# Expert up products from rounded parts and rests, with a re-ordered drain and routing chain

## The chip, the cores and the metric

One core of a Trainium2 chip. The metric is the device time of one execution in microseconds (us). An execution's time is its span, from the first to the last instruction, and a little around it.

## What is computed

A decoder layer in float32 for x of 16 batches x 256 tokens x 256 features:

1. Stage A: causal self-attention (16 heads, relative position bias, RMS norms) with a ReLU network 256-1024-256.
2. Stages B and D: attention to a context (8 heads, layer norms), then a second ReLU network, 256-1024-256, in stage D.
3. Stage C: each of the 4096 tokens takes the nearest of 8 centroids, and goes through that expert alone:

```python
xn = rms_norm(x)
ids = argmin(dist2(xn, centroids))
h = xn @ up_w[e]                   # 256 -> 1024, e the token's expert
a, g = split(h, 2)                 # 512 each
y = (a * silu(g)) @ down_w[e]      # 512 -> 256
out = y + x
```

## The kernel before

The kernel is written per engine: each engine has its own queue, run in order, and semaphores order them against each other. Phase 1 is a software pipeline over the batches: `PHASES` (line 131) lists turns, and in one turn stage A works on one batch, B on the one before, D on the one before that, C on the one before that. Within a turn the order of the attention pieces is the list `PLAN` (lines 77 to 81), which every engine walks, skipping the stages that its turn hasn't got. The last turns have fewer stages: B + 1 has B, D, C; B + 2 has D and C (D of batch 15, C of batch 14); B + 3 has C alone. These three are the drain.

What matters of the drain, by engine. VectorE: `rest` (L1122) makes the second part of a value, the difference between it and its rounded copy; D.out is taken at L1335 and goes through statistics (L1134, L1137), scaling (L1344, L1350), statistics again; the scaled rows begin at L1269; `nearest` (from L1181 to L1194) picks the expert. ScalarE: L737 rounds D's input (`d_qT_hi`), `hidden` (L754, L755) takes the hidden halves of D's network from PSUM, `scaled_rows` (L729) stands between its second and third call. GpSimd: `layer_then_rms` (L933 to L955) computes two norms from the statistics in ten operations of 2 elements. TensorE: D's hidden products are made from rounded parts and rests already (`split_cols_out`): with w = w_hi + w_low and x = x_hi + x_low, three single-pass products x_hi w_hi, x_hi w_low, x_low w_hi stand for one product in float32, which takes two passes. Eight eighths of D.out ("out", and two after the plan) share PSUM bank 5 with D.h2, so the first waits for the third `hidden`.

The experts' weights (8 x 1 MB up, 8 x 0.5 MB down) are loaded in turn B + 1, into the room of stage A.

Routing follows the drain: GpSimd makes counters (L1020 to L1024), VectorE runs a chain of small operations on the experts of all 4096 tokens (L1429 to L1473), in which every step waits for the one before, and TensorE sorts the tokens by expert with one-hot products: `in_row` (L1459) says which row in a tile a token takes, `in_tile` (L1455) which tile, and `number` (GpSimd L1030, ScalarE L867) is what is sorted. All three engines first wait for `phase1_over`: the last expert chosen and the last rows stored.

The expert stage has 39 tiles of 128 tokens, two a step, in 19 steps and one lone tile. For a tile GpSimd gathers the rows (L1035), TensorE transposes them (L1844), ScalarE copies them from PSUM (L871), TensorE makes the up products in two halves of 512 columns (`up_half`, in float32), ScalarE takes Silu of one half (L876), VectorE multiplies by the other (L1482), TensorE transposes the hidden values (L1869), ScalarE copies them (L878), TensorE makes the down products, VectorE adds the token's own row (L1493), and GpSimd scatters the result (L1056). `product` (L1505) records nearly all matrix products, so tiles and not lines tell them apart.

Of the kernel before, what the change touches and what calls it, by code (L numbers as in the profile page):

```python
# [31 lines left out]
P = 128  # L32
# [7 lines left out]
E = 8  # L40
# [40 lines left out]
PLAN += [("out", "D", 5), ("weigh", "B", 1), ("norm", "A", 0), ("norm", "A", 1), ("norm", "B", 0), ("norm", "B", 1)]  # L81

# [84 lines left out]
def _build(nc, d, ctx):  # L167
# [77 lines left out]

    b_kh, b_kl, b_qh, b_ql = (sbuf(ctx, name, [P, C, S], F32R) for name in ("b_kh", "b_kl", "b_qh", "b_ql"))
# [6 lines left out]
    def carver():  # L253

        at = [0]
# [21 lines left out]
    w1o = p1("w1o", [P, C, D])  # L277
    w11 = p1("w11", [P, C, HID])
    w12 = p1("w12", [P, J, D])
# [8 lines left out]

    rec = p1("rec", [P, 3, S])
    rec_few = p1("rec_few", [P, 16])  # L290
    x1 = p1("x1", [P, T, D])

    c_in = p1("c_in", [P, T, D])
    b_ctxT = p1("b_ctxT", [P, C, S])
    b_xl = p1("b_xl", [P, T, D])
    b_xT = p1("b_xT", [P, C, S])


    b_v = p1("b_v", [P, T, D])
    b_nm = p1("b_nm", [P, T, C, 4, 32])  # L300
    b_p = p1("b_p", [P, NPB, T, S])
    b_zT = p1("b_zT", [P, C, S])
    b_yT = p1("b_yT", [P, C, S])
    b_q = p1("b_q", [P, T, D])
    b_hT = p1("b_hT", [P, J, S])
# [211 lines left out]
    s_route, s_pp, s_wmoe = map(sem, ("routing_chain", "prefixes_made", "experts_loaded"))  # L517
# [13 lines left out]
    pr.close()  # L531
    up = sbuf(ctx, "up", [P, E, C, 2 * EH])
    down = sbuf(ctx, "down", [P, E, EJ, D])
    p3 = carver()
    m_row = p3("m_row", [P, 2, 2, 1], U32)
    m_token = p3("m_token", [P, 2, 1], U32)
    m_in = p3("m_in", [P, 2, D])
    m_skip = p3("m_skip", [P, 2, D])
    m_xT = p3("m_xT", [P, 2, C, P])
    m_sg = p3("m_sg", [P, 2, EH])  # L540
    m_h = p3("m_h", [P, 2, EH])
    m_hT = p3("m_hT", [P, 2, EJ, P])
    m_out = p3("m_out", [P, 2, D])
    oh = p3("oh", [P, NT, E])
    r_pp = p3("r_pp", [P, NT, E])
# [17 lines left out]
    r_id = p3("r_id", [P, 4, TILES_MAX])  # L563
    io_p = p3("io_p", [P, 1])
    io_r = p3("io_r", [P, P])
    io_n = p3("io_n", [P, NT])
    io_e = p3("io_e", [P, E])
    io_t = p3("io_t", [P, NT])
    io_i = p3("io_i", [P, TILES_MAX])
    tri = p3("tri", [P, P])  # L570
    ones_nt = p3("ones_nt", [P, NT])
    s_iota, s_numbered = sem("iotas_made"), sem("one_hot_numbered")
    BY_TILE = {"m_loaded": 16, "m_skip": 16, "m_row": 1, "m_x": 1, "m_xT": 1, "m_up": 1, "m_silu": 1,
# [33 lines left out]
    def _(sp):  # L607
# [23 lines left out]
        def load_experts():  # L631

            after(sp, "b_xl", B - 1)
            for e in range(E):
                sp.dma_start(up[:, e], w_view(d["L0_ffn_up_w"][e])).then_inc(s_wmoe, 16)
                sp.dma_start(down[:, e], w_view(d["L0_ffn_down_w"][e])).then_inc(s_wmoe, 16)
# [47 lines left out]
    def _(act):  # L684
# [29 lines left out]

        def evacuate(it, job, dst, view=None):

            src = full(act, it, job)[:]
            copy(dst, src if view is None else view(src)).then_inc(e_sem(job), 1)  # L718

        def turn(it):  # L720
# [83 lines left out]
            for what, st, n in PLAN:  # L804
                if st not in it.stages:
                    continue
                if what == "lengths":
                    after(act, "c_rows", c, T)
                    for t in range(T):
                        nc.scalar.activation(b_zT[:, t], c_rows[:, t, 0:D], ACT.Square,  # L810
# [56 lines left out]
        nc.scalar.activation(number[:, :, 1], in_tile[:], ACT.Copy, scale=io_p[:, 0:1]).then_inc(s_numbered, 1)  # L867
# [22 lines left out]
    def _(pool):  # L890
# [125 lines left out]
        phase1_over(pool)  # L1016
        for io, pattern, base, by_partition in (
# [12 lines left out]
        pool.tensor_tensor(number[:, :, 0], in_tile[:], io_n[:].unsqueeze(2).to_broadcast([P, NT, TILES_MAX]),  # L1030
                           ALU.mult).then_inc(s_numbered, 1)
# [7 lines left out]
        pool.wait_ge(s_route, ROUTE_ALL)  # L1039
        for u in range(2):  # L1040
# [30 lines left out]
    def _(dve):  # L1071
# [101 lines left out]
        def turn(it):  # L1173
# [57 lines left out]
            if Dd:  # L1231
# [56 lines left out]
            for what, st, n in PLAN:  # L1288
# [127 lines left out]
        phase1_over(dve)  # L1416
        dve.wait_ge(s_iota, 8)
# [56 lines left out]
        assert link[0] == ROUTE_ALL  # L1474

# [469 lines left out]
```

## Time and profile before

| | us |
|---|---|
| runs (3) | 1348.08, 1350.71, 1352.39; median 1350.71 |
| profiled execution, its own time | 1350.49 |
| span of the profiled execution | 1348.80 |
| TensorE busy in the span | 1223.9 (91%) |
| VectorE, ScalarE, GpSimd busy | 811.2, 611.4, 413.7 |
| mean granted clock of TensorE, share of full | 0.959 |

PE is TensorE, PEld its weight loads, DVE VectorE, ACT ScalarE, POOL GpSimd. In a row, "128x512 f32<-128x512 f32" is output and input shape, "x4" how many instructions a row merges, and the bracket says how long the engine had been idle and who released it. Times are from the start of the span.

### The profile page before, as it was taken

What the parts mean: (1) busy time and instruction counts of PE and PEld (TensorE: products, weight loads), DVE (VectorE), ACT (ScalarE), POOL (GpSimd) and SP (SyncE); (2) the same over time, 40 slices, a digit from 0 to 9 for tenths busy, and PEclk for the clock granted to TensorE, in tenths of its full rate; (3) what the DMA queues carried; (4) which work ended last, traced back from release to release, by engine and by line L of the source; (5) the groups of instructions that cost most, each with busy time, mean ns of one, the idle gap of its engine ahead of it and who ended that gap; (6) DMA issues with size and microseconds to landing.
All of it is one profiled execution on the core that took longest, in us unless ns stands there. A gap on an engine that the chain in (4) does not pass through costs nothing.

```text
span 1348.8 us, 29314 instructions
## 1 busy us (share of the span) xinstructions
PE 1223.9 (91%) x9542; PEld 915.5 (68%) x9543; DVE 811.2 (60%) x2110; ACT 611.4 (45%) x1288; POOL 413.7 (31%) x712
## 2 busy tenths in 40 slices
PE   6497999999999999999999999999985289999997
PEld 4274778778787877878787787878765145555554
DVE  3737667777786877778687777877644611211211
ACT  3426456464746646474654647465442122222211
POOL 1310324233142423314142331414122234444352
PEclk9598999999999999999999999999998589999998
DMA  8402520303213030321303032130383012121121
GB/s 265 126 1 110 222 107 17 111 16 109 80 52 117 16 109 16 109 80 48 121 16 109 16 109 77 48 124 9 111 324 113 16 49 64 51 62 53 55 66 28
DMA packets 51768, 112.29 MB, mean 83 GB/s; under 512 B 7333, under 2 KB 38863, under 8 KB 44944
## 3 DMA queue, kind: packets, MB, share of 16 engines
q1 hardware_dynamic: 45456, 96.81, 21.3%
q0 software_dynamic: 5616, 14.43, 3.6%
q10 hardware_dynamic: 656, 0.52, 0.1%
q8 instruction: 24, 0.39, 0.1%
q14 instruction: 16, 0.13, 0.0%
HBM read 89.72 MB, written 22.94 MB: 84 GB/s over the span
## 4 chain that ended last, share of the span: by engine, by line
PE 76%; DVE 10%; ACT 6%; issue 5%; DMA 2%; POOL 1%; SPq 0%; DVEq 0%; ACTq 0%; POOLq 0%
PE bank L1505 69%; PE bank L1540 3%; DVE a_p L1295 2%; PE bank L1706 2%; ACT shared L823 2%; PE bank L1869 1%; DMA rows_skip<-shared 1%; ACT shared L878 1%; ACT a_p L818 1%; DVE b_ql L1199 1%; DVE a_split L1227 1%; DVE a_split L1226 1%; DVE a_split L1225 1%; DVE a_ss L1236 1%; ACT a_sq L741 1%
## 5 line engine op out<-in xcount | busy, mean ns | idle before, releaser
L1505 PE MATMUL bank<-shared 128*128 128x256 f32 (+4 forms) x1730 | 320.3, 376 | 27.6 <-POOL shared L1030 11.3
L1505 PEld LDWEIGHTS bank<-shared 128*128 128x128 f32 (+2 forms) x1730 | 219.8, 166 | 88.7 <-issue 31.7
L1295 DVE TENSOR_TENSOR a_p<-a_p,eb 128x385 f32<-128x385 f32 x256 | 125.9, 555 | 75.6 <-ACT a_p L818 75.6
L1505 PE MATMUL bank<-up,shared 128*128 x312 | 143.8, 604 | 11.1 <-issue 11.1
L991 POOL TENSOR_SCALAR a_rz<-a_ms 128x2 f32<-128x2 f32 x16 | 3.1, 191 | 407.5 <-ACT a_sq L842 407.5
L818 ACT ACTIVATE a_p<-bank 128x385 f32<-128x385 f32 x256 | 105.1, 504 | 44.3 <-PE bank L1505 44.2
L1482 DVE TENSOR_TENSOR shared<-bank,shared 128x512 f32<-128x512 f32 x39 | 27.0, 692 | 153.7 <-ACT shared L876 153.7
L1505 PEld LDWEIGHTS bank<-up,shared 128*128 128x128 f32 x312 | 56.9, 192 | 75.6 <-issue 75.6
L876 ACT ACTIVATE shared<-bank 128x512 f32<-128x512 f32 x39 | 23.3, 597 | 137.2 <-PE bank L1505 137.2
L1505 PE MATMUL bank<-down,shared 128*128 x312 | 76.8, 390 | 7.2 <-ACT shared L878 7.2
L823 ACT ACTIVATE shared<-bank 128x512 f32<-128x512 f32 x128 | 66.1, 603 | 35.3 <-PE bank L1505 35.3
L1262 DVE TENSOR_REDUCE shared<-bank 128x2 f32<-128x512 f32 x128 | 79.4, 684 | 1.3 <-PE bank L1505 1.3
L1505 PEld LDWEIGHTS bank<-down,shared 128*128 128x128 f32 x312 | 58.2, 192 | 27.2 <-issue 20.9
L971 POOL TENSOR_TENSOR a_split<-a_sq,a_split 128x256 f16<-128x256 f32 x64 | 42.8, 699 | 104.6 <-ACT a_split L772 104.6
L1035 POOL DMA_INDIRECT shared<-rows_x,shared x35 | 33.1, 945 | 112.1 <-PE bank L1844 107.0
L1505 PE MATMUL bank<-a_p,a_v 128*32 128x256 f32 (+1 forms) x1024 | 58.5, 347 | 8.0 <-DVE a_p L1295 6.2
L1505 PE MATMUL bank<-w_low,a_hT_hi 128*128 128x256 f32 x224 | 63.4, 283 | 0.0
L1505 PE MATMUL bank<-w_hi,a_hT_hi 128*128 128x256 f32 x224 | 62.9, 281 | 0.0
L1505 PE MATMUL bank<-d_qT_hi,w_hi 128*128 128x256 f32 x256 | 57.4, 306 | 5.8 <-DVE d_qT_low L1122 5.8
L1505 PE MATMUL bank<-w_hi,a_hT_low 128*128 128x256 f32 x224 | 62.4, 279 | 0.0
L1505 PE MATMUL bank<-w0qk,a_xnT 128*128 128x512 f32 x128 | 61.1, 621 | 0.7 <-ACT a_xnT L718 0.7
L927 POOL TENSOR_TENSOR shared<-shared,mhalf 128x2 f32<-128x2 f32 x80 | 56.3, 704 | 12.7 <-POOL shared L959 6.6
(237 smaller groups left out, 2724.8 us busy)
## 6 DMA issues: line engine op xcount, KB each, us to landing
w_low<-low_w SPq DMA_DIRECT2D x44, 1024.0 KB, 4.8
up<-in_L_ffn_up_w SPq DMA_DIRECT2D x8, 1024.0 KB, 13.9
x_in<-in_x SPq DMA_DIRECT2D x16, 256.0 KB, 2.7
shared<-in_ctx SPq DMA_DIRECT2D x16, 256.0 KB, 3.1
rows_x<-shared SPq DMA_DIRECT2D x16, 256.0 KB, 5.8
rows_skip<-shared SPq DMA_DIRECT2D x16, 256.0 KB, 6.2
down<-in_L_ffn_down_w SPq DMA_DIRECT2D x8, 512.0 KB, 12.3
toep<-a_hT SPq DMA_DIRECT2D x1, 3072.0 KB, 10.2
```

The costliest lines, as they stand in the source:

```text
L818: nc.scalar.activation(a_p[:, head % NPA], ps[:, 0:SCOLS], ACT.Exp).then_inc(e_sem(f"A.s{head}"), 1)
L823: nc.scalar.activation(b_p[:, head % NPB].rearrange("p t s -> p (t s)"), ps[:], ACT.Exp).then_inc(e_sem(f"B.s{head}"), 1)
L876: nc.scalar.activation(m_sg[:, u], bank[3 + 2 * u][:], ACT.Silu).then_inc(mig[u]["m_silu"], 1)
L927: pool.tensor_tensor(out, in_, mhalf[:, 0:out.shape[-1]], ALU.pow).then_inc(sig[name], 1)
L971: ins = pool.tensor_tensor(a_split[:, t, H0:, slot, :], hat[:, H0:], a_split[:, t, H0:, 0, :], ALU.subtract)
L1035: pool.indirect_dma_start(out=dst[:, u], out_offset=None, in_=src.ap(), in_offset=bass.IndirectOffsetOnAxis(ap=rows, axis=0)).then_inc(mig ...
L1262: dve.tensor_reduce(b_nm[:, n // 4, :, n % 4, 0:1], ps[:].rearrange("p (m s) -> p m s", s=S), AX_X, ALU.max, negate=True).then_inc(e_sem(f ...
L1295: tt(a_p[:, n_ % NPA], a_p[:, n_ % NPA], eb[:, n_], ALU.mult).then_inc(sig["a_p"], 1)
L1482: tt(m_h[:, u], bank[2 + 2 * u][:], m_sg[:, u], ALU.mult).then_inc(mig[u]["m_h"], 1)
L1505: return mm(out, lhsT=lhsT, rhs=rhs, start=first, stop=last, **kw)
L1540: ins = nc.tensor.transpose(ps[:, c * S + t * P:c * S + (t + 1) * P], x[:, t, c * P:(c + 1) * P], ident[:])
L1706: ins = nc.tensor.transpose(ps[:, g * P:(g + 1) * P], a_split[:, t, h:h + 2].rearrange("p h s d -> p (h s d)"), ident16[:])
```

## The change

- Every up weight is kept as a rounded part `up_hi` and a rest `up_low`, the latter in the place of the weights. ScalarE rounds (`round_up_weights`), VectorE subtracts (`rest_of_up`, in halves of 128 x 1024). The parts for experts 0 to 2 are rounded at the start of turn B + 2, 3 to 6 at its end, 7 after D.out; the rests of experts 0 to 3 stand in VectorE's turn B + 2 between `nearest` and D.out, 4 and 5 after the last statistics of that turn, 6 and 7 after the routing chain.
- Each tile's transposed rows become `m_xhi` (ScalarE) and `m_xlow` (VectorE), and an up half is six products of rounded operands in place of two in float32.
- The rest of D's input for batch 15 moves from the start of turn B + 2 to turn B + 1, ahead of D.out of batch 14.
- Turn B + 2 walks `DRAIN_PLAN`, with the distances behind the third and fourth eighth of D.out.
- The counters have memory of their own and no longer wait for the end of phase 1; VectorE's routing waits for the last expert only, GpSimd's gathers for the stores.
- One-hot rows are made token column by token column (32 operations, 128 x 128 float16) rather than in four; `number` comes in two halves.
- Memory of phase 1 is laid out in another order, so that `up_hi` finds room.

```diff
+DRAIN_PLAN = [("lengths", "C", 0), ("out", "D", 0), ("out", "D", 1), ("rows", "C", 0), ("out", "D", 2), ("out", "D", 3)]
+DRAIN_PLAN += [("distances", "C", 0), ("expert", "C", 0), ("out", "D", 4), ("out", "D", 5)]
+def plan_of(turn):
+    return DRAIN_PLAN if turn.first == B + 2 else PLAN
...
+        def round_up_weights(which):
+            for e in which:
+                act.wait_ge(s_up[e], 16)
+                copy(flat(up_hi[:, e]), flat(up[:, e])).then_inc(s_up_hi, 1)
...
             if Dd:
                 copy(flat(d_qT_hi[:]), full(act, it, "D.q")[:]).then_inc(sig["d_qhi"], 1)
+            if it.first == B + 2:
+                after(act, "x1_kept", B - 1)
+                round_up_weights(range(3))
...
+            if it.first == B + 2:
+                after(act, "c_nx", c)
+                round_up_weights(range(3, E - 1))
+                taken(act, it, "D.out")
+                round_up_weights(range(E - 1, E))
...
-            copy(m_xT[:, u].rearrange("p c s -> p (c s)"), bank[u][:, 0:C * P]).then_inc(mig[u]["m_xT"], 1)
+            copy(flat(m_xhi[:, u]), bank[u][:, 0:C * P]).then_inc(mig[u]["m_xT"], 1)
...
-        phase1_over(pool)
...
+        pool.tensor_copy(io_r16[:], io_r[:]).then_inc(s_iota, 1)
...
+        for half in range(2):
+            part = slice(half * NT // 2, (half + 1) * NT // 2)
+            pool.tensor_tensor(number[:, part, 0], in_tile[:, part],
+                               io_n[:, part].unsqueeze(2).to_broadcast([P, NT // 2, TILES_MAX]),
+                               ALU.mult).then_inc(s_numbered[half], 1)
...
         pool.wait_ge(s_route, ROUTE_ALL)
+        phase1_over(pool)
...
+        def rest_of_up(halves):
+            for n in halves:
+                e, c_ = n // C, n % C
+                if c_ == 0:
+                    dve.wait_ge(s_up_hi, e + 1)
+                ins = tt(up_low[:, e, c_], up[:, e, c_], up_hi[:, e, c_].bitcast(F32), ALU.subtract)
+            ins.then_inc(s_up_low, len(halves) // C)
...
-            if Dd:
+            if Dd and it.first != B + 2:
                 rest(it, "D.q", d_qT_low[:], d_qT_hi[:], "d_qhi")
...
+            if it.first == B + 1:
+                rest(Turn(it.phase + 1, 0), "D.q", d_qT_low[:], d_qT_hi[:], "d_qhi")
...
+            if it.first == B + 2:
+                rest_of_up(range(0, 8))
             if Dd:
                 ps = full(dve, it, "D.out")
...
+            if it.first == B + 2:
+                rest_of_up(range(8, 12))
...
-        phase1_over(dve)
-        dve.wait_ge(s_iota, 8)
+        after(dve, "c_expert", B - 1)
+        dve.wait_ge(s_iota, 9)
...
-            chain(tt(in_row[:, part], bc(r_place[:, 1, part], P), over(io_r[:], NT // QUARTERS, P), ALU.is_equal))
+            for n in range(part.start, part.stop):
+                ins = ts(in_row[:, n], io_r16[:], r_place[:, 1, n:n + 1], None, ALU.is_equal)
+            chain(ins)
...
+        rest_of_up(range(12, 16))
+        def rest_of_rows(k, u):
+            after_tile(dve, "m_xT", k, u)
+            tt(flat(m_xlow[:, u]), bank[u][:, 0:C * P], flat(m_xhi[:, u]).bitcast(F32), ALU.subtract
+               ).then_inc(mig[u]["m_xl"], 1)
+        for u in range(2):
+            rest_of_rows(0, u)
...
                 tt(m_out[:, u], bank[DOWN_BANK[u]][:, 0:D], m_skip[:, u], ALU.add).then_inc(mig[u]["m_out"], 1)
+                if u == 0:
+                    for v in range(nxt):
+                        rest_of_rows(k + 1, v)
...
-        pe.wait_ge(s_wmoe, 16 * 2 * E)
+        pe.wait_ge(s_wmoe, 16 * E)
+        pe.wait_ge(s_up_low, E)
...
-            def up_half(u, half):
-                for c in range(C):
-                    w = up[:, bass.ds(expert[u], 1), c, half * EH:(half + 1) * EH]
-                    ins = product(bank[2 + 2 * u + half][:], m_xT[:, u, c], w.rearrange("p o n -> p (o n)"),
-                                  c == 0, c == C - 1)
+            def up_half(u, half, x_low_new):
+                for x, w_part in ((m_xhi, up_hi), (m_xhi, up_low), (m_xlow, up_hi)):
+                    if x is m_xlow and x_low_new:
+                        after_tile(pe, "m_xl", k, u)
+                    for c in range(C):
+                        w = w_part[:, bass.ds(expert[u], 1), c, half * EH:(half + 1) * EH]
+                        ins = product(bank[2 + 2 * u + half][:], x[:, u, c], w.rearrange("p o n -> p (o n)"),
+                                      c == 0 and x is m_xhi and w_part is up_hi, c == C - 1 and x is m_xlow)
```

## Rows read from the trace of the kernel before

**Rows 1.** The page, section 4: shares of the chain that ended last, by engine.

```profile
PE 76%; DVE 10%; ACT 6%; issue 5%; DMA 2%; POOL 1%; SPq 0%; DVEq 0%; ACTq 0%; POOLq 0%
```

**Rows 2.** Stretches: start:end, us, then busy us (instructions) per engine, clock, DMA, GB/s.

```profile
1022.00:1026.00 4.00, 1.60 (x7) 1.60 (x8) 2.31 (x7) 0.00 (x0) 1.75 (x6) 0.50 0.00 0
...
1257.40:1270.50 13.10, 12.16 (x44) 7.24 (x44) 2.62 (x11) 2.92 (x6) 5.89 (x7) 1.00 0.17 51
```

**Rows 3.** Timeline, one pair: start us, us, engine, line, op, out<-in, xcount [idle before].

```profile
1257.42 5.41 PE L1505 MATMUL bank<-up,shared 128*128 x12 [0.60 <-issue]
...
1262.67 0.60 PE L1869 MATMUL bank<-ident,shared 128*128 128x128 f32 x4
...
1264.83 1.89 PE L1505 MATMUL bank<-down,shared 128*128 x8
...
1266.56 0.60 PE L1869 MATMUL bank<-ident,shared 128*128 128x128 f32 x4
...
1267.03 0.42 DVE L1493 TENSOR_TENSOR shared<-bank,shared 128x256 f32<-128x256 f32 x1
...
1267.92 1.99 PE L1505 MATMUL bank<-down,shared 128*128 x8 [0.33 <-ACT shared L878]
...
1270.56 0.69 PE L1505 MATMUL bank<-up,shared 128*128 x1 [0.65 <-issue]
```

**Rows 4.** Timeline of TensorE, D.h of batch 15, three of its rows of two.

```profile
1026.70 0.63 PE L1505 MATMUL bank<-d_qT_low,w_hi 128*128 128x256 f32 x2
...
1027.92 0.40 PE L1505 MATMUL bank<-d_qT_hi,w_hi 128*128 128x256 f32 x2
...
1031.22 0.40 PE L1505 MATMUL bank<-d_qT_low,w_hi 128*128 128x256 f32 x2
```

**Rows 5.** Timeline of ScalarE and of VectorE, weights rounded and parted at the start.

```profile
130.00 1.93 ACT L713 CAST made<-w 128x2048 fp32r<-128x2048 f32 x1
...
134.49 2.28 DVE L1111 TENSOR_TENSOR a_hT_low<-w,a_hT_low 128x2048 fp32r<-128x2048 f32 x1
```

**Rows 6.** Timeline of the drain, batches 14 and 15, all engines.

```profile
1017.82 0.68 DVE L1335 TENSOR_TENSOR shared<-bank,shared 128x512 f32<-128x512 f32 x1
...
1018.66 0.58 ACT L737 CAST d_qT_hi<-bank 128x512 fp32r<-128x512 f32 x1 [8.70 <-PE bank L1540]
...
1023.67 0.67 DVE L1122 TENSOR_TENSOR d_qT_low<-bank,d_qT_hi 128x512 fp32r<-128x512 f32 x1
...
1027.55 2.96 DVE L1269 SCALAR_TENSOR_TENSOR shared<-shared 128x256 f32<-128x256 f32 x2 [3.20 <-POOL shared L955]
...
1031.83 1.99 PE L1505 MATMUL bank<-shared 128*128 128x256 f32 x8 [0.22 <-ACT shared L755]
...
1036.99 0.17 DVE L1194 CAST expert_of<-shared 128x2 f32<-128x2 uint32 x1
...
1041.38 0.69 DVE L1335 TENSOR_TENSOR shared<-bank,shared 128x512 f32<-128x512 f32 x1 [4.22 <-PE bank L1505]
...
1046.58 0.30 DVE L1137 BATCH_NORM_AGGREGATE shared<-shared 128x2 f32<-128x6 f32 x2
...
1050.68 0.88 DVE L1269 SCALAR_TENSOR_TENSOR shared<-shared 128x256 f32<-128x256 f32 x2 [3.80 <-POOL shared L955]
```

**Rows 7.** Timeline of the routing, all engines.

```profile
1056.88 0.17 DVE L1194 CAST expert_of<-shared 128x2 f32<-128x2 uint32 x1
...
1059.27 0.43 DVE L1429 TENSOR_TENSOR shared<-expert_of,shared 128x256 f32<-128x256 f32 x1 [2.21 <-POOL shared L1024]
...
1069.70 6.97 DVE L1459 TENSOR_TENSOR shared<-shared 128x1024 f16<-128x1024 f32 x4
...
1069.82 3.25 POOL L1030 TENSOR_TENSOR shared<-shared 128x1248 f16<-128x1248 f32 x1 [10.68 <-DVE shared L1455]
...
1079.10 0.18 DVE L1473 CAST sorted_row<-shared 128x39 uint32<-128x39 f32 x1
...
1082.78 0.66 PE L1844 MATMUL bank<-ident,shared 128*128 128x128 f32 x2 [5.36 <-DMA shared<-rows_x,sorted_row]
```

More of the change, by code:

```diff
@@ L251, in _build, with carver @@
     place = {}
-    def carver():
-        at = [0]
+    def carver(first=0):
+        at = [first]
         def carve(name, shape, dt=F32):
@@ L277, in _build @@
     w1o = p1("w1o", [P, C, D])
+    rec = p1("rec", [P, 3, S])
+    rec_few = p1("rec_few", [P, 16])
+    x1 = p1("x1", [P, T, D])
+    c_in = p1("c_in", [P, T, D])
+    b_ctxT = p1("b_ctxT", [P, C, S])
+    b_xl = p1("b_xl", [P, T, D])
+    b_xT = p1("b_xT", [P, C, S])
+    b_v = p1("b_v", [P, T, D])
+    b_nm = p1("b_nm", [P, T, C, 4, 32])
     w11 = p1("w11", [P, C, HID])
+    b_p = p1("b_p", [P, NPB, T, S])
+    b_zT = p1("b_zT", [P, C, S])
+    b_yT = p1("b_yT", [P, C, S])
+    b_hT = p1("b_hT", [P, J, S])
     w12 = p1("w12", [P, J, D])
@@ L514, in each @@
                     body(Turn(phase, k))
-    s_route, s_pp, s_wmoe = map(sem, ("routing_chain", "prefixes_made", "experts_loaded"))
+    s_route, s_pp, s_wmoe = map(sem, ("routing_chain", "prefixes_made", "down_weights_loaded"))
+    s_up = [sem(f"up_weights_loaded{e}") for e in range(E)]
+    s_up_hi, s_up_low = sem("up_weights_rounded"), sem("up_weights_rest_made")
     pa.close()
@@ L531, in _build @@
     pr.close()
+    under_up = ExitStack()
+    up_low = sbuf(under_up, "up_low", [P, E, C, 2 * EH], F32R)
+    under_up.close()
     up = sbuf(ctx, "up", [P, E, C, 2 * EH])
     down = sbuf(ctx, "down", [P, E, EJ, D])
[L534 to L543, printed above, removed]
+    m_xhi = sbuf(ctx, "m_xhi", [P, 2, C, P], F32R)
+    m_xlow = sbuf(ctx, "m_xlow", [P, 2, C, P], F32R)
+    UP_HI_END = E * C * 2 * EH - 5 * C * S
+    p3 = carver(UP_HI_END)
+    r_id = p3("r_id", [P, 4, TILES_MAX])
+    moe = carver(UP_HI_END + 160)
+    m_row = moe("m_row", [P, 2, 2, 1], U32)
+    m_token = moe("m_token", [P, 2, 1], U32)
+    m_in = moe("m_in", [P, 2, D])
+    m_skip = moe("m_skip", [P, 2, D])
+    m_sg = moe("m_sg", [P, 2, EH])
+    m_h = moe("m_h", [P, 2, EH])
+    m_hT = moe("m_hT", [P, 2, EJ, P])
+    m_out = moe("m_out", [P, 2, D])
     oh = p3("oh", [P, NT, E])
-    r_pp = p3("r_pp", [P, NT, E])
     r_tot = p3("r_tot", [P, NT, E])
@@ L560, in _build @@
     number = p3("number", [P, NT, 2, TILES_MAX], F16)
[L563 to L573, printed above, removed]
+    io_p = sbuf(ctx, "io_p", [P, 1])
+    io_r = sbuf(ctx, "io_r", [P, P])
+    io_n = sbuf(ctx, "io_n", [P, NT])
+    io_e = sbuf(ctx, "io_e", [P, E])
+    io_t = sbuf(ctx, "io_t", [P, NT])
+    io_i = sbuf(ctx, "io_i", [P, TILES_MAX])
+    io_r16 = sbuf(ctx, "io_r16", [P, P], F16)
+    tri = sbuf(ctx, "tri", [P, P])
+    ones_nt = sbuf(ctx, "ones_nt", [P, NT])
+    s_iota, s_numbered = sem("iotas_made"), [sem(f"one_hot_numbered{half}") for half in range(2)]
+    BY_TILE = {"m_loaded": 16, "m_skip": 16, "m_row": 1, "m_x": 1, "m_xT": 1, "m_xl": 1, "m_up": 1, "m_silu": 1,
                "m_h": 1, "m_ht": 1, "m_hT": 1, "m_down": 1, "m_out": 1, "m_stored": 16}
@@ L803, in turn @@
                 evacuate(it, "B.max", b_nmT[:].rearrange("p c s -> p (c s)"))
-            for what, st, n in PLAN:
+            for what, st, n in plan_of(it):
                 if st not in it.stages:
@@ L809, in turn @@
                     for t in range(T):
-                        nc.scalar.activation(b_zT[:, t], c_rows[:, t, 0:D], ACT.Square,
+                        junk = b_f if it.first == B + 3 else b_zT
+                        nc.scalar.activation(junk[:, t], c_rows[:, t, 0:D], ACT.Square,
                                              accum_out=c_nx[:, t:t + 1]).then_inc(sig["c_nx"], 1)
@@ L866, in _ @@
         act.wait_ge(s_route, ROUTE_IN_TILE)
-        nc.scalar.activation(number[:, :, 1], in_tile[:], ACT.Copy, scale=io_p[:, 0:1]).then_inc(s_numbered, 1)
+        for half in range(2):
+            part = slice(half * NT // 2, (half + 1) * NT // 2)
+            nc.scalar.activation(number[:, part, 1], in_tile[:, part], ACT.Copy, scale=io_p[:, 0:1]
+                                 ).then_inc(s_numbered[half], 1)
         def transposed(k, u):
             after_tile(act, "m_x", k, u)
-            copy(m_xT[:, u].rearrange("p c s -> p (c s)"), bank[u][:, 0:C * P]).then_inc(mig[u]["m_xT"], 1)
+            copy(flat(m_xhi[:, u]), bank[u][:, 0:C * P]).then_inc(mig[u]["m_xT"], 1)
         def step(k, n, nxt, nxt2):
@@ L1028, in _ @@
         pool.wait_ge(s_iota, 8)
+        pool.tensor_copy(io_r16[:], io_r[:]).then_inc(s_iota, 1)
         pool.wait_ge(s_route, ROUTE_IN_TILE)
-        pool.tensor_tensor(number[:, :, 0], in_tile[:], io_n[:].unsqueeze(2).to_broadcast([P, NT, TILES_MAX]),
-                           ALU.mult).then_inc(s_numbered, 1)
+        for half in range(2):
+            part = slice(half * NT // 2, (half + 1) * NT // 2)
+            pool.tensor_tensor(number[:, part, 0], in_tile[:, part],
+                               io_n[:, part].unsqueeze(2).to_broadcast([P, NT // 2, TILES_MAX]),
+                               ALU.mult).then_inc(s_numbered[half], 1)
         def gather(dst, src, rows, name, u):
@@ L1287, in turn @@
                 low_parts((0,))
-            for what, st, n in PLAN:
+            for what, st, n in plan_of(it):
                 if st not in it.stages:
@@ L1735, in out_eighth @@
                     ins.then_inc(f_sem("D.out"), 1)
-            for what, st, n in PLAN:
+            for what, st, n in plan_of(it):
                 if st not in it.stages:
```

31 lines of the change are left out of this document (11 added, 20 removed).

## The prediction

> **What bounds the kernel now.** I read the page's chain first: TensorE holds 76% of it [rows 1]. I then cut the span by stage, since the change touches only two: the expert stage (from 1085 us to the end) and the drain ahead of it (1017 to 1085 us), and read both as timelines.
>
> In the expert stage a pair of tiles takes 1270.56 - 1257.42 = 13.14 us, of which TensorE is busy 12.16 at full granted clock [rows 2, 3]. Up products are 16 of the 44 records: an fp32 product leaves two records, one per pass, and in the run of 12 they start every (5.41 - 0.69) / 11 = 0.43 us. So a 512-column up product costs 0.86 us, and a pair has 8 of them: 6.9 of 13.1 us.
>
> In the drain TensorE mostly waits. The chain goes from engine to engine: D.out, two norms on VectorE and GpSimd, the scaled rows on ScalarE, the transposes, the distances, the expert's choice, then the routing chain on VectorE [rows 6, 7]. There an instruction added to VectorE costs time wherever the chain isn't elsewhere.
>
> **The expert stage.** Each fp32 up product becomes three rounded ones: 24 instead of 16 records a pair. Their price isn't in the trace at 512 columns. Two rows bound it. A rounded 256-column product starts every (1031.22 - 1027.92) / 28 = 0.118 us, 14 rows of two in that stretch [rows 4]; two of them would be 0.236. An fp32 pass over 256 columns takes (1266.56 - 1264.83) / 8 = 0.216 us [rows 3]; since the rounded product is about twice as quick per column, 512 rounded columns occupy the array as long as one such pass. I take 0.216 (the nearer row: same array time per instruction), with 0.236 as the far end and 0.213 as the near one (512 columns at the upper clock level of 2.4 GHz).
>
> Not all of the saving lands. The order is up of tile 0 (12 products now), up of half of tile 1 (6), transposes of tile 0's hidden, the other half of tile 1 (6), down of tile 0. From the end of tile 0's up (1257.42 + 8 x 0.43 = 1260.86) through Silu, the gating multiply and the weight load to those transposes at 1262.67 there are 1.81 us; the half of tile 1 filled 1.72 of it. It shrinks to 6 x 0.216 = 1.30, but the hand-off stays 1.81, so TensorE waits about 0.5 us, and that half saves nothing. On the path: 12 x 0.43 = 5.16 becomes 18 x 0.216 = 3.89, a saving of 1.27 a pair. The second hand-off, tile 1's Silu and multiply, is still covered by the 1.73 us of tile 0's down. The rest of the period (1.36 from the second transposes to down of tile 1, then 2.64 to the next pair) is unchanged. 19 pairs x 1.27 = 24.1, plus the lone last tile's 8 x 0.43 - 12 x 0.216 = 0.85: **25.0 us less**. At 0.236: 19 x 0.91 + 0.6 = 17.9; at 0.213: 26.
>
> The rows' rests are new on VectorE: two operations of 256 elements from PSUM a pair, 0.42 us each like the output's [rows 3], put right after tile 0's output. VectorE is busy 2.62 of 13.1 us [rows 2], it waits there for down of tile 1, and the rests are wanted only at the fifth product of the next pair. I cost them at nothing; uncovered they would be 0.84 us a pair. The slack of GpSimd's six transfers a pair shrinks by 1.3 us, but GpSimd is busy only 5.9 of 13.1 [rows 2].
>
> **The drain, step by step.**
> 1. The rest of D.q (batch 15) goes ahead of D.out of batch 14 on VectorE. It waits for ScalarE's copy, which ends at 1018.66 + 0.58 = 1019.24, and takes 0.67 [rows 6]; D.out of 14 starts near 1019.9 instead of 1017.82. A store wait of 0.4 further down is absorbed, so its norm chain is **1.6 us** later. TensorE's D.h start 4 us earlier, and gain nothing: the last of the hidden halves stand behind the scaled rows of batch 14 on ScalarE, and D.out needs the bank that they free. D.out starts at 1031.83 + 1.6.
> 2. ScalarE rounds three experts ahead of the hidden halves: 3 x 1.93 = 5.8 us from 1019.24 [rows 5], done by 1025.1; scaled rows come after 1029. Hidden; with no cover, up to 5.8.
> 3. TensorE then stands idle some 5 us before D.out. In 1022 to 1026, where it had been idle too (busy 1.60 of 4.00), the granted clock was 0.50, the lower level of 1.2 GHz [rows 2], and two rounded products still took 0.63 instead of 0.40 at 1026.70 [rows 4]. I charge **1.3** (0 to 1.5). The distances now stand behind two more eighths of D.out: **0.6**. The choice of expert for batch 14 ends at 1036.99 + 0.17 + 1.6 + 1.3 + 0.6 = 1040.7.
> 4. Only then VectorE parts four experts: eight halves of 2.28 / 2 = 1.14 us each [rows 5], 9.1 us, up to 1049.8. These stand ahead of D.out of batch 15, whose products are done near 1043. It began at 1041.38, after 4.22 us of idleness [rows 6]. So **+8.4**: the 9.1 us are hidden only in part.
> 5. Two more experts are parted (4.6 us) between the last statistics (1046.58 + 0.30) and the next VectorE step at 1050.68, where GpSimd's ten small operations run, 3.8 us [rows 6]. Alone that costs 0.7. But a VectorE operation with two SBUF operands and a GpSimd one block each other here: the pair of L1269 that took 0.88 us at 1050.68 took 2.96 beside GpSimd's multiplications at 1027.55, and four one-hot quarters took 6.97 beside GpSimd's 3.25 us [rows 6, 7]. If each half lets one small operation through, the first four of the ten are pushed out to 5.9 us and the other 2.1 follow: 8.0 instead of 3.8, **+4.2**.
>
> The Trainium skill ("SBUF — State Buffer", Who interferes with whom) says the same as those rows: the pair of ports that VectorE and GpSimd share is locked for a whole instruction. It adds that a tensor_scalar may enter a mode that takes both ports, while writing DMA descriptors isn't held up by tensor_tensor. The first speaks against the one-hot rows of step 7, the second for the rests of step 8; no row here shows either. With both taken at the page's word the sum of the drain would be 11.9.
>
> 6. The iotas and the wait for batch 15's stores leave the path: 1059.27 - 1057.05 = **2.2 less** [rows 7].
> 7. One-hot rows: four operations (6.97 us, 2.0 of it blocked) become 32 short ones. Their price is unseen: between 0.1 and 0.25 us each, or 3.5 to 8, and GpSimd's numbering (now two halves) may block them twice. What follows is the same, so -3.5 to +1.1; I take **-0.5**, the blocked case being the nearer row.
> 8. The last two experts (4.6 us) stand between the last routing step (1079.28) and the first transposes, 3.5 us later [rows 7]; the rests of the first rows follow. 0.4 to 2.5, I take **+1**.
>
> Sum of the drain: 8.4 + 4.2 - 2.2 - 0.5 + 1 = **10.9 us more**; bounds 2.5 (no lower clock, no blocking, cheap rows) and 14.
>
> The profiled execution took 1350.49 (span 1348.80 and 1.69 around it), 0.2 under the median of 1350.71. 1350.5 - 25.0 + 10.9 = **1336 us**.
>
> **Rivals.**
> - No blocking on the shared port. Step 5 costs 0.7, step 7 gives 2.1, step 8 costs 0.4: drain +5.2, 1331 us. For: the ten GpSimd operations have two elements each, and none of them is seen beside such a long VectorE operation. Against: the two blocked rows.
> - A rounded 512-column product costs 0.236: 1350.5 - 17.9 + 10.9 = 1344. For: the 256-column ones are 0.01 above half of the fp32 pass, whatever that is; against: a cost per instruction wouldn't double with the columns.
> - Slower: the products become bound by their addresses. Each up product takes its weights at the expert's register, so the queue of TensorE computes an address for each, three times as many as now. With t per product, 19 x 18 + 12 = 354 on the path give 354 x (0.287 - t); the gain is eaten by the drain at t = 0.256. At 0.30 the time would be 1350.5 + 4.7 + 10.9 = 1366. For: nothing now runs at under 0.43 per address. Against: between 1267.92 and 1270.56 the queue computed three such addresses, read two expert numbers and took the loop's branch, with only 0.65 idle [rows 3].
> - The rests are covered on both sides but the drain takes all (no change): step 4 would have to cost 22 us, for which VectorE's rows leave no room.
>
> **How the numbers follow.** Forecast 0.55, no blocking 0.22, 0.236 a product 0.10, address-bound 0.08, the rest between. The range runs from 1324 (26 saved, drain near its lower bound) to 1347 (17.9 saved, drain at 14). A difference of 0.3%, 4 us, is what this measurement can tell from no change; the first three cases are all faster: 0.87 faster, 0.06 the same, 0.07 slower.
>
> **What would show it.** Up products of 0.216 apart in threes and a pair of 11.9 us with 0.5 us of TensorE waiting for VectorE ahead of the hidden transposes; D.out of batch 15 on VectorE near 1050, right behind the eight halves; GpSimd's small operations after it stretched by about 4 us; the routing's first step at once after the choice; first up products near 1096. A pair of 13 us or more would overturn the forecast, and so would halves that run before the distances are in.

## The result, and the profile after

The changed kernel takes **1356.49 us** (median of 6 runs, 1356.03 to 1358.61); the kernel before, beside it, 1349.53 (1347.57 to 1352.45). The ratio is 1.005, 95% interval 1.0033 to 1.0067: slower by half a per cent, where 1336 us were forecast. The profiled execution took 1358.28 us, span 1356.5, against 1348.8 before.

Code that is alike up to the drain reaches it up to 6 us earlier or later from one execution to the next (the scaled rows of batch 14 started between 1024.5 and 1030.9 us in the profiles of this study). So parts are compared by their lengths; only the drains of before and after stand 0.14 us apart (the copy of D.q at 1018.66 and 1018.52) and can be read against each other as they are. From the first transposes of hidden rows to the last ones before took 1339.24 - 1092.35 = 246.9 us, after 1346.49 - 1103.93 = 242.6. The expert stage gave back **4.3 us of the 25.0 forecast**; the drain cost about what was forecast.

TensorE's share of the page's chain is 73%, against 76% before [rows 1].

Two stretches (start:end, us, busy us (instructions) of TensorE, its weight loads, VectorE, ScalarE, GpSimd, then clock, DMA, GB/s). The first is the one where TensorE had stood idle [rows 2]; D.h fills it now. The second is one pair of tiles:

```profile
1022.00:1026.00 4.00, 4.00 (x29) 3.87 (x27) 2.65 (x8) 3.97 (x6) 1.11 (x3) 0.81 0.02 4
1201.75:1214.69 12.94, 11.25 (x52) 8.56 (x53) 3.34 (x12) 2.82 (x6) 5.83 (x7) 1.00 0.20 58
```

TensorE is busy 11.25 us of the pair in place of 12.16, but the pair still takes 12.94 in place of 13.14. The timeline of that pair (start us, us, engine, line, operation, out<-in, count [idle before <- releaser]) shows where the rest went; it answers to [rows 3]:

```profile
1201.75 0.73 PE L1578 MATMUL bank<-up_hi,m_xhi 128*128 x2 [0.65 <-issue]
...
1205.97 0.97 POOL L1077 DMA_INDIRECT shared<-rows_skip,shared  x1 [0.30 <-issue]
...
1206.16 0.66 PE L1947 MATMUL bank<-ident,shared 128*128 128x128 f32 x4
...
1206.57 0.70 PE L1578 MATMUL bank<-up_hi,m_xhi 128*128 x2
...
1208.16 0.58 ACT L917 COPY shared<-bank 128x512 f32<-128x512 f32 x1 [2.79 <-PE bank L1947]
1208.65 0.60 ACT L915 ACTIVATE shared<-bank 128x512 f32<-128x512 f32 x1
...
1208.89 1.99 PE L1578 MATMUL bank<-down,shared 128*128 x8 [0.69 <-ACT shared L917]
...
1210.72 0.60 PE L1947 MATMUL bank<-ident,shared 128*128 128x128 f32 x4
```

The rounded products come every 0.227 us (ten of them from 1202.31 to 1204.58). The transposes of tile 0's hidden rows start at 1206.16. Their copy out of the bank starts only at 1208.16, **2.0 us behind them**, and it is TensorE's signal that is late: the trace has the semaphore that the copy waits for raised 1.99 us behind the start of the transposes. Tile 0's down products wait 0.69 us for it, and Silu of tile 1, behind that copy on ScalarE, starts when the copy is done. Tile 1's transposes then come 4.56 us behind tile 0's, against 3.89 in before [rows 3], though the products between are shorter. In before the same copy came 0.64 us behind its transposes of 1262.67 [rows 3], the semaphore 0.61 behind, with the residual gather of tile 1 just issued:

```profile
1261.69 0.97 POOL L1035 DMA_INDIRECT shared<-rows_skip,shared  x1 [0.30 <-issue]
...
1263.31 0.58 ACT L878 COPY shared<-bank 128x512 f32<-128x512 f32 x1 [1.56 <-PE bank L1869]
```

In every pair of before that delay is 0.63 to 0.64. In after it is 0.69 to 0.70 in the first pair, the last pair and the lone tile, and 1.59 to 2.48 in the 17 pairs between (the expectations below count them as 18). In all 17 GpSimd is issuing tile 1's residual gather beside or just ahead of the transposes (here 1205.97 to 1206.94), and the copy starts 1.20 to 1.30 us after that issue ends, wherever the issue lies against the transposes. This was the lead for the experiments.

The lone last tile of the same run differs. A scatter is in issue until 0.18 us behind the start of its transposes, and its copy isn't late (0.69), though a pair whose issue ended at 0.36 had a delay of 1.59:

```profile
1345.66 1.01 POOL L1099 DMA_INDIRECT out_rows<-shared  x1 [0.30 <-issue]
...
1346.49 0.66 PE L1947 MATMUL bank<-ident,shared 128*128 128x128 f32 x4 [1.41 <-DVE shared L1552]
1347.19 0.58 ACT L917 COPY shared<-bank 128x512 f32<-128x512 f32 x1 [1.48 <-PE bank L1947]
```

It has rounded products ahead of its transposes, with 1.41 us of idleness between, and only fp32 ones behind them (the down products, from 1347.91).

The drain and the routing, answering to [rows 6, 7]:

```profile
1019.81 0.68 DVE L1391 TENSOR_TENSOR shared<-bank,shared 128x512 f32<-128x512 f32 x1
...
1029.09 2.90 DVE L1321 SCALAR_TENSOR_TENSOR shared<-shared 128x256 f32<-128x256 f32 x2 [3.79 <-POOL shared L994]
...
1041.07 0.17 DVE L1246 CAST expert_of<-shared 128x2 f32<-128x2 uint32 x1
1041.15 9.16 DVE L1162 TENSOR_TENSOR up_low<-up,up_hi 128x1024 fp32r<-128x1024 f32 x8
1050.23 0.68 DVE L1391 TENSOR_TENSOR shared<-bank,shared 128x512 f32<-128x512 f32 x1
...
1055.64 4.60 DVE L1162 TENSOR_TENSOR up_low<-up,up_hi 128x1024 fp32r<-128x1024 f32 x4
1055.81 1.10 POOL L972 TENSOR_SCALAR shared<-shared 128x2 f32<-128x2 f32 x1 [2.80 <-DVE shared L1189]
1056.99 1.53 POOL L966 TENSOR_TENSOR shared<-shared,mhalf 128x2 f32<-128x2 f32 x1
...
1062.45 0.88 DVE L1321 SCALAR_TENSOR_TENSOR shared<-shared 128x256 f32<-128x256 f32 x2 [2.21 <-POOL shared L994]
...
1068.64 0.17 DVE L1246 CAST expert_of<-shared 128x2 f32<-128x2 uint32 x1
1068.85 0.43 DVE L1487 TENSOR_TENSOR shared<-expert_of,io_e 128x256 f32<-128x256 f32 x1
...
1079.28 7.69 DVE L1518 TENSOR_SCALAR shared<-io_r,shared 128x128 f16<-128x128 f16 x32
...
1089.41 0.18 DVE L1533 CAST sorted_row<-shared 128x39 uint32<-128x39 f32 x1
1089.62 4.63 DVE L1162 TENSOR_TENSOR up_low<-up,up_hi 128x1024 fp32r<-128x1024 f32 x4
1089.90 2.08 POOL L1077 DMA_INDIRECT shared<-rows_x,sorted_row  x1 [8.07 <-DVE sorted_row L1533]
...
1094.51 0.66 PE L1919 MATMUL bank<-ident,shared 128*128 128x128 f32 x2 [6.78 <-DVE up_low L1162]
```

The 32 narrow one-hot rows alone, in two stretches (start:end, us, VectorE's busy us (instructions of L1518), clock, DMA, GB/s); GpSimd's two numbering operations take 2.49 us from 1079.34 on:

```profile
1079.28:1081.79 2.51, 2.51 (x3) 0.50 0.02 7
1081.79:1086.97 5.18, 5.08 (x30) 0.50 0.00 0
```

The second count has the end of the third row in it once more.

### The profile page after: what moved, and what is told of

Same layout as the page of the kernel before. It is cut to its first block, busy times and chain, and to the rows that moved or that the text cites. A ratio compares the mean times of both kernels' runs of the same rounds, so it can differ in the third digit from the quotient of the medians.

```text
span 1356.5 us, 29880 instructions
## 1 busy us (share of the span) xinstructions
PE 1208.9 (89%) x9698; PEld 945.9 (70%) x9699; DVE 845.1 (62%) x2193; ACT 624.3 (46%) x1297; POOL 417.6 (31%) x714
## 4 chain that ended last, share of the span: by engine, by line
PE 73%; DVE 11%; ACT 6%; issue 6%; POOL 1%; DMA 1%; another core or an unknown queue 0%; DVEq 0%; SPq 0%; ACTq 0%; POOLq 0%
PE bank L1578 65%; PE bank L1947 3%; PE bank L1613 3%; DVE a_p L1347 2%; PE bank L1779 2%; ACT shared L854 2%; ACT shared L917 2%; ACT a_p L849 1%; DVE up_low L1162 1%; DVE b_ql L1251 1%; DVE a_split L1278 1%; DVE a_split L1279 1%; DVE a_split L1277 1%; DVE a_ss L1288 1%; DVE shared L1518 1%
## 5 line engine op out<-in xcount | busy, mean ns | idle before, releaser
L917 ACT COPY shared<-bank 128x512 f32<-128x512 f32 x39 | 22.8, 585 | 91.1 <-PE bank L1947 87.9
L1578 PE MATMUL bank<-up_hi,m_xhi 128*128 x156 | 53.0, 421 | 11.0 <-issue 11.0
```

The costliest lines, as they stand in the source:

```text
L917: copy(m_hT[:, u].rearrange("p j s -> p (j s)"), bank[H_BANK[u]][:]).then_inc(mig[u]["m_hT"], 1)
L1578: return mm(out, lhsT=lhsT, rhs=rhs, start=first, stop=last, **kw)
```

## The experiments

Each ratio is to the kernel before on the same chip, with its 95% interval. "Delay" is the time from the start of tile 0's hidden transposes to their copy.

**1. The gathers left out (no_later_skip).** VectorE's wait for them goes with them.

```diff
-                if u < nxt:
-                    gather(m_skip, rows_skip, m_row[:, 1, u], "m_skip", u)
```

> The kernel after, without the residual gathers of all pairs but the first (later tiles add the first pair's rows). Open: in 18 pairs of after the copy of tile 0's turned hidden rows starts 1.6 to 2.5 us after the transposes began, in every pair of before 0.63. Theory 'gather': TensorE's signal behind these transposes is held back while GpSimd issues tile 1's residual gather; it came 1.18 to 1.27 us after that issue ended in all 18. Then the copy here starts 0.64 to 0.70 behind the transposes; down(0) starts when up(1,0) ends (T+1.8 in place of T+2.7), the period of a pair falls from 13.0 to about 12.0 us, and 18 pairs give 17 us: 1337 to 1341 us. Theory 'order': rounded products right behind fp32 transposes hold the signal back, whatever GpSimd does: copy still 2.0 behind, period 13.0, 1354 to 1357 us.

Measured: delay 0.69 to 0.70 in every pair, period 12.0 us, 225.9 us from the first hidden transposes to the last: as the gather's theory has it. The time is not: 1348.20 us (1341.25 to 1352.49), ratio 0.998 (0.9961 to 1.0002). In the profile the span ends 8.1 us behind the last scatter's issue, in experiment 3 it is 2.7; why the last rows land late here isn't shown.

**2. The kernel before with the gather beside its transposes (before_late_gathers).**

```diff
+                if u == 0 and nxt:
+                    pool.tensor_tensor(ones[:, 0:2], ones[:, 2:4], mhalf[:, 0:2], ALU.pow).then_inc(mig[0]["m_late"], 1)
+                    after_tile(pool, "m_late", k, 0)
```

> The kernel before, with one two-element power operation on GpSimd (0.70 us) in each pair ahead of the scatters, so that tile 1's residual gather ends about 0.8 us after the hidden transposes begin, as in after. 'Gather' alone, whatever the products are: the copy of tile 0 starts about 1.9 us behind its transposes here too, down(0) 0.5 us later, 18 pairs: about 1359 us. If the held signal needs the rounded products as well as the gather: copy 0.64 behind, 1350 us as before. 'Order': 1350 us.

Measured: 1349.49 us, ratio 1.0003 (0.9987 to 1.0019). In the second pair, shown here, the whole issue lies over the transposes. In most others the added operation pushes the transfers further than intended: a scatter is in issue until 0.2 us behind the start of the transposes, and the gather from 0.5 to 1.5 behind it. The copy comes 0.64 us behind in all of them:

```profile
1102.32 0.97 POOL L1035 DMA_INDIRECT shared<-rows_skip,shared  x1 [0.30 <-issue]
1102.42 0.60 PE L1872 MATMUL bank<-ident,shared 128*128 128x128 f32 x4
...
1103.06 0.58 ACT L878 COPY shared<-bank 128x512 f32<-128x512 f32 x1 [1.56 <-PE bank L1872]
```

So a transfer in issue is not enough: among fp32 products nothing is held.

**3. The gather put off (skip1_after_up).**

```diff
                 if u < nxt:
+                    if u == 1:
+                        after_tile(pool, "m_up", k + 1, 1)
                     gather(m_skip, rows_skip, m_row[:, 1, u], "m_skip", u)
```

> The kernel after; GpSimd issues tile 1's residual gather only when the next pair's up products of tile 1 are done (about 2.1 us behind tile 0's hidden transposes); nothing is left out. 'Gather': the copy of tile 0 starts 0.64 to 0.7 behind, period about 12.0 us, 1337 to 1341 us if the gather then holds back nothing; if every TensorE signal within 1.2 us of an issue is held, tile 1's transposes are late by some 0.3 to 0.9 us a pair in turn and the time is 1344 to 1355. 'Order': 1354 to 1357.

Measured: **1340.93 us**, ratio 0.9943 (0.9923 to 0.9962), period 12.0, 225.8 us between the first and the last hidden transposes in place of 242.6. One wait on GpSimd gives 16.8 us (the stage as after has it took 242.7, 241.0 and 239.2 us in the profiles of experiments 7, 8 and 10, so this is good to some 3 us). The delay is 0.69 to 0.78 in all pairs but one: in the 18th, where a scatter's issue ends only 0.04 us ahead of the transposes, it is 1.12. The gather now lies over tile 1's transposes, which stand between fp32 products and fp32 transposes, and these are not held (0.63):

```profile
1152.71 0.66 PE L1949 MATMUL bank<-ident,shared 128*128 128x128 f32 x4
...
1153.43 0.59 ACT L917 COPY shared<-bank 128x512 f32<-128x512 f32 x1 [1.50 <-PE bank L1949]
...
1155.62 0.97 POOL L1077 DMA_INDIRECT shared<-rows_skip,shared  x1 [3.36 <-PE bank L1580]
...
1156.31 0.60 PE L1949 MATMUL bank<-ident,shared 128*128 128x128 f32 x4
...
1156.94 0.59 ACT L917 COPY shared<-bank 128x512 f32<-128x512 f32 x1 [1.57 <-PE bank L1949]
```

**4. The gather right behind the transposes' signal (skip1_after_turn).** The same edit with `"m_ht", k + 1, 0` as what is waited for.

> After with tile 1's residual gather issued as soon as tile 0's hidden transposes have signalled (0.7 to 1.7 us behind their start). If each TensorE signal that falls into an issue or the 1.2 us behind it is held, the signal of tile 1's up products (2.06 behind in after) waits until about 2.9: Silu(1), its multiply and its transposes 0.85 later, of which tile 0's down products cover nothing: about 0.8 a pair, 1352 to 1356 us. If only the signal of transposes is held: 1339 to 1343.

Measured: 1338.99 us, ratio 0.9921 (0.9896 to 0.9947). Silu of tile 1 starts at 1189.43, inside the issue, on the signal of rounded products whose last two began at 1188.78. That signal is not held, as the transposes' was in after:

```profile
1188.05 0.59 ACT L917 COPY shared<-bank 128x512 f32<-128x512 f32 x1 [1.48 <-PE bank L1949]
...
1188.88 0.97 POOL L1077 DMA_INDIRECT shared<-rows_skip,shared  x1 [2.01 <-PE bank L1949]
...
1189.43 0.60 ACT L915 ACTIVATE shared<-bank 128x512 f32<-128x512 f32 x1 [0.80 <-PE bank L1580]
```

**5. A scatter in the gather's place (scatter_last).** Tile 1's gather is issued ahead of its scatter instead of behind it.

> After with tile 1's residual gather issued ahead of its scatter, so that the gather ends 0.5 us before tile 0's hidden transposes begin and a scatter is in issue beside them. If gathers alone hold TensorE's signal (to 1.2 us behind their end): held by 0.1 us at most, period 12.0, 1339 to 1343 us. If any indirect transfer in issue holds it: copy 1.2 behind the scatter's end, 1354 to 1358.

Measured: 1356.28 us, ratio 1.0063 (1.0039 to 1.0086). Delay 2.03 in the pair shown, 1.59 to 2.48 in 17; the copy starts 1.27 behind the end of the scatter's issue (1.21 to 1.33 in 17). It isn't the gather as such; a scatter in issue does the same:

```profile
1139.48 1.01 POOL L1101 DMA_INDIRECT out_rows<-shared  x1 [0.30 <-issue]
...
1139.73 0.66 PE L1949 MATMUL bank<-ident,shared 128*128 128x128 f32 x4
...
1141.76 0.58 ACT L917 COPY shared<-bank 128x512 f32<-128x512 f32 x1 [2.80 <-PE bank L1949]
```

**6. An fp32 transposition in between (one_more_turn).**

```diff
                 ins.then_inc(mig[u]["m_ht"], 1)
+                if u == 0 and n == 2:
+                    nc.tensor.transpose(bank[DOWN_BANK[0]][:, D:D + P], ident[:], ident[:])
```

> After with one more fp32 transposition (of the identity, into an unused part of a bank) between tile 0's hidden transposes and the rounded products behind them; GpSimd's gathers where after has them. If the signal is held because a rounded product follows the transposes directly, the fp32 one in between frees it: copy 0.64 to 0.75 behind, 18 times 0.9 us less and 0.11 more: 1340 to 1344 us. If it is held by the rounded products anywhere behind (or ahead) with a gather in issue: copy still 1.2 us behind the issue's end, 1355 to 1359 us.

Measured: 1353.48 us, ratio 1.0023 (1.001 to 1.0037). The time lies between the two ranges. The copy still waits (1.99 at the pair of 1165 us, 1.15 behind the issue's end; 1.09 to 1.18 in 15 of 17 pairs, 0.45 and 0.42 in the other two). A rounded product directly behind the transposes is not what it takes.

**7. The rests spread over idle places, four on GpSimd (rests_moved).** Halves 0 to 5 go behind the scaled rows of 14, 6 and 7 stay, 8 and 9 go behind the scaled rows of 15, 10 and 11 behind the one-hot, and on GpSimd:

```diff
+        for n in range(12, 16):
+            e, c_ = n // C, n % C
+            ins = pool.tensor_tensor(up_low[:, e, c_], up[:, e, c_], up_hi[:, e, c_].bitcast(F32), ALU.subtract)
```

> The kernel after with the sixteen rests of the up weights spread: six behind the scaled rows of batch 14 (VectorE idle from 1032 to 1040), two behind the choice of 14, two behind the scaled rows of batch 15, two behind the one-hot, four on GpSimd. Theory 'queue' (the drain is late by the rests that stand on VectorE's way): the addition of D's output of 15 comes at about 1043.7 in place of 1050.2, the choice of 15 ends at about 1059.4 in place of 1068.8, the first rows start 2.3 earlier on top: 1343 to 1347 us. Rival 'port': the rests beside GpSimd's chain and GpSimd's own two-operand rests block each other wherever they stand: the choice of 15 ends at 1064 or later, 1350 us or more.

Measured: 1351.64 us, ratio 1.0033 (1.0018 to 1.0047): the time is the rival's. The choice of 15 ends 33.7 us behind the scaled rows of 14, between the two (39.7 in after). The queue's theory holds for VectorE's own halves, the port's for those on GpSimd. Beside GpSimd's four, two 8-element additions (0.36 us in after) took 4.61, and the one-hot comparison (0.43) took 2.52:

```profile
1052.63 10.21 POOL L1069 TENSOR_TENSOR up_low<-up,up_hi 128x1024 fp32r<-128x1024 f32 x4
...
1053.66 4.61 DVE L1238 TENSOR_SCALAR shared<-shared 128x8 f32<-128x8 f32 x2
...
1060.60 2.52 DVE L1494 TENSOR_TENSOR shared<-expert_of,io_e 128x256 f32<-128x256 f32 x1
```

**8. The rests in VectorE's gaps, none on GpSimd (rests_in_gaps),** the last four at the end of routing as in after:

> The drain's half of that kernel alone. Theory: of the 10 us that the first tiles are late in after, all is the place of the rests in VectorE's queue. The choice of 15 then ends about 27.5 us behind the scaled rows of 14 (39.8 in after) and the first Silu comes about 62.4 behind them (73.5 in after, 63.3 in before): 1344 to 1348 us. Rival: the rests take their time wherever they stand, since VectorE or the shared port is the bound: first Silu 68 or more behind, 1350 or more.

Measured: 1344.47 us, ratio 0.9938 (0.9917 to 0.9959). From the scaled rows of 14 to the first hidden transposes: 65.2 us, against 74.8 in after and 64.8 in before. The first Silu comes 63.9 us behind (62.4 expected). 9.6 us of the drain's loss were the places of the ten halves that were moved (6 and 7 and the last four stay).

**9. Both repairs (gaps_and_skip1).**

> After with both repairs: tile 1's residual gather issued behind the next pair's up products of tile 1 (18 pairs at 12.0 us in place of 13.0), and the rests in VectorE's gaps: six behind the scaled rows of batch 14, two behind its choice, two behind the scaled rows of 15, two behind the one-hot, four at the end of routing as in after, none on GpSimd. If the two losses of after are independent, they add: 15.5 us from the gathers and about 11 from the drain: 1327 to 1332 us. If the earlier first tile shifts the gathers back onto the transposes or the drain's loss is only handed on to the routing, 1335 to 1341.

Measured: **1333.42 us**, ratio 0.9859 (0.9836 to 0.9882), just above the range. It is 23.1 us under after, where the two repairs alone gave 15.6 and 12.0; the intervals don't tell this from a plain sum. Six halves run where VectorE waited for the distances, and the addition of batch 15 waits for TensorE again. The four at the end still end what TensorE waits for ahead of the first row transposes:

```profile
1030.87 2.87 DVE L1323 SCALAR_TENSOR_TENSOR shared<-shared 128x256 f32<-128x256 f32 x2 [3.81 <-POOL shared L994]
...
1033.67 7.96 DVE L1164 TENSOR_TENSOR up_low<-up,up_hi 128x1024 fp32r<-128x1024 f32 x6
...
1046.67 0.69 DVE L1397 TENSOR_TENSOR shared<-bank,shared 128x512 f32<-128x512 f32 x1 [0.24 <-PE bank L1583]
...
1088.09 0.66 PE L1924 MATMUL bank<-ident,shared 128*128 128x128 f32 x2 [6.78 <-DVE up_low L1164]
```

**10. Before's wide one-hot operations (rows_by_tensor_tensor).**

```diff
-            for n in range(part.start, part.stop):
-                ins = ts(in_row[:, n], io_r16[:], r_place[:, 1, n:n + 1], None, ALU.is_equal)
-            chain(ins)
+            chain(tt(in_row[:, part], bc(r_place[:, 1, part], P), over(io_r[:], NT // QUARTERS, P), ALU.is_equal))
```

> After with the one-hot rows made by before's four tensor-tensor operations of float32 in place of 32 tensor-scalar ones of float16. If the 32 are no cheaper (7.69 us in after for an expected 3.5 to 7), the four take about 7.0 and GpSimd's half of the numbers runs late again behind the shared port (3 us or more); the end moves by less than 1 us: 1355 to 1357. If the 32 are held by GpSimd's two numbering operations, they are the slower only for the first 2.5 us.

Measured (one run, 1353.13 us, under the range): four operations in 6.83 us where the 32 took 7.69, although GpSimd's numbers take 4.44 beside them and 2.49 beside the 32. From the one-hot to the sorted rows 19.9 us instead of 20.7. The last case of the expectation is what after shows: there the 32 lose 2.0 us to GpSimd's numbers, all of it in the first 2.5 us.

```profile
1078.21 6.83 DVE L1517 TENSOR_TENSOR shared<-shared,io_r 128x1024 f16<-128x1024 f32 x4
1078.26 4.44 POOL L1071 TENSOR_TENSOR shared<-shared,io_n 128x624 f16<-128x624 f32 x2 [15.50 <-DVE shared L1513]
```

The expert stage is shorter here too, 239.2 us. Two of its 17 pairs, at 1229.68 and 1267.49, have the gather's issue where the others have it and aren't held:

```profile
1229.50 0.98 POOL L1077 DMA_INDIRECT shared<-rows_skip,shared  x1 [0.30 <-issue]
1229.68 0.66 PE L1945 MATMUL bank<-ident,shared 128*128 128x128 f32 x4
...
1230.37 0.59 ACT L917 COPY shared<-bank 128x512 f32<-128x512 f32 x1 [1.47 <-PE bank L1945]
```

**11. All three (three_repairs).**

> The kernel with both repairs, and before's four wide operations for the one-hot rows, which were 0.86 us shorter than the 32 narrow ones and brought the sorted rows 0.87 earlier behind the choice. If that stays: 0.9 us under the kernel with two repairs (1333.4), 1331 to 1334, faster than before by 1.4%. If GpSimd's numbers, slower beside the wide ones (4.44 us against 2.49), hold up the last one-hot products: no gain, 1333 to 1335.

Measured: **1330.05 us**, ratio 0.9865 (0.9843 to 0.9887), 1.35% under before. With the ninth it is the fastest of this study; the ratios are alike, so the third edit gained nothing that can be told. One pair there, in the columns of the stretches above, is 12.01 us long:

```profile
1145.30:1157.31 12.01, 10.95 (x54) 8.62 (x53) 3.35 (x12) 2.92 (x6) 5.91 (x7) 1.00 0.21 62
```

## Why the prediction was wrong

**The step that failed** is the expert stage's "On the path: 12 x 0.43 = 5.16 becomes 18 x 0.216 = 3.89, a saving of 1.27 a pair", with down of tile 0 following the second half of tile 1 at once, as before. It was worked out as if only the products' lengths changed. The shorter products also bring the hidden transposes forward against GpSimd's six transfers, which start from the pair before: in 15 of the 19 pairs of before the last issue ended 0.01 to 0.13 us ahead of the transposes; in after it ends 0.7 to 0.8 behind their start in as many. The prediction did look at GpSimd, but at its busy time (5.9 of 13.1 us), not at what its issues would then lie beside. So tile 0's down doesn't follow at once: the copy that it needs waits for a signal that comes up to 1.8 us late, and a pair takes 13.0 us in place of 11.9.

Of the 25.0 us, 24.1 were forecast between the first and the last hidden transposes (the first tile's products stand ahead of them), and 4.3 came there. 16.8 are the held signal (242.6 - 225.8, shown by experiment 3, which moves nothing but that gather). The product's price took 3.9: 19 pairs x 18 x (0.2275 - 0.216) = 3.9. That price lies inside the bounds given (0.213 to 0.236). Together this is 0.9 us more than is missing, less than the stage varies from profile to profile.

What holds the signal is narrowed to two conditions. One is an indirect transfer of GpSimd in issue at or just ahead of the transposes; 1, 3 and 4 take it away by itself, and 5 shows that a scatter does as well. The other is rounded products around these fp32 transposes: 2 has fp32 ones, but it is the kernel before and differs in more than that, and tile 1's transposes in 3 stand among fp32 work. The lone last tile speaks against the rounded products ahead of the transposes and for those behind, but TensorE is idle there on both sides, so this isn't shown. Nor are the two conditions always enough: in the six profiles that have both (after, 5, 6, 7, 8, 10), the copy came 1.09 to 1.33 us behind the issue's end in 98 of 102 pairs, and earlier in four. By what path GpSimd's issue reaches TensorE's signal stays open. The Trainium skill ("SBUF — State Buffer", Who interferes with whom) says that "PE and ACT never wait on anyone". The trace agrees for the instructions: the products behind the transposes run on at 0.23 us each. It is the transposes' signal that comes late, by up to 1.8 us, and of signals the sentence says nothing.

**The drain**, step by step.
- Step 1 was right: D.out of 14 at 1019.81 (forecast 1019.9), scaled rows of 14 1.5 later (1.6).
- Steps 2 and 3 were right: the roundings stayed hidden, the choice of 14 ended at 1041.24 (1040.7). The lower clock cost a little more than the 1.3 charged: D.out's first eight products took 3.78 us at a granted clock of 0.50, against 1.99 before [rows 6].
- Step 4 was right, 8.85 instead of 8.4: the eight halves took 9.16 us, and the addition of batch 15 came at 1050.23 (1049.8).
- Step 5 had the right mechanism, too large. GpSimd's small operations were stretched beside the halves (1.10, 1.53, 0.55 and 1.05 us where 0.22, 0.71, 0.20 and 0.20 are usual), as one of them after each half. The chain took 6.73 us, not 8.0, against 3.80 before: +2.9 instead of +4.2.
- Step 6 was right: the one-hot starts at once behind the choice.
- Step 7 had the wrong sign: +0.7, not -0.5. The last 29 of the 32 narrow rows take 5.18 us, 0.18 each, inside the 0.1 to 0.25 allowed. Of the first three, two are held up for one of GpSimd's numbering operations each, so that the three take 2.51 us. The prediction allowed for two such blocks; at 2.0 us they cost as much as the single one in the kernel before. The Trainium skill's rule of step 7 ("SBUF — State Buffer", Who interferes with whom), that a tensor_scalar may take both ports, agrees with these two and with the additions of experiment 7. GpSimd went first here, and its numbers took 2.49 us beside the narrow rows, 4.44 beside the wide ones.
- Step 8 was 1.4 instead of 1. The Trainium skill's other rule there (the same section), that tensor_tensor doesn't hold up the writing of descriptors, doesn't hold here: the first two gathers took 2.08 and 1.67 us to issue beside the halves, 1.25 and 0.96 without them (experiment 7, and before).

At the first row transposes after stands 1094.51 - 1082.78 = 11.7 us behind before; 10.9 were forecast. That the sum is so close is in part luck: step 5 was 1.3 too large, steps 7 and 8 together 1.6 too small.

**The rivals.** "A pair of 13 us or more would overturn the forecast": it did, with 14 of the 19 periods at 12.87 to 13.16. The rival that came out slower, products bound by their addresses, isn't the cause: they came every 0.227 us, under its deciding 0.256. The rival at 0.236 a product was half right on the price and wrong on the time. Port blocking was there, in steps 5 and 7, where it was charged.

## What to carry to other kernels

When a change shortens one engine's stretch of a loop, lay the other engines' issues over the new period, those with slack too: ask what each will now run beside. If a loop's period shrinks less than its work, look at the delay from an operation's start to its reader's start, pair by pair, and at what else ended a constant time before. New work on a shared engine belongs where that engine waits; here other places for 10 of the 16 new operations were worth 9.6 us.

## What the runs showed of the hardware

- The signal of fp32 transposes between rounded products was held until 1.2 us (1.18 to 1.27 in 17 pairs of after) after a GpSimd indirect transfer, gather or scatter, had been issued; four of 102 such pairs were held less or not at all. The signal of rounded products, and that of transposes among fp32 products, was not held.
- A rounded 512-column product with a new weight load came every 0.227 us at full clock, against 0.86 for fp32.
- Two VectorE tensor_scalar operations of 8 elements, 0.36 us elsewhere, took 4.61 us beside GpSimd's two-operand subtractions. Of 32 of 128x128 float16, two took 1.23 and 1.27 us beside GpSimd's numbering operations (1.30 and 1.23), the others about 0.25.
- Two indirect gathers took 2.08 and 1.67 us to issue beside VectorE's two-operand subtractions, 1.25 and 0.96 without them.
